# A new written order of five engines' work in the prologue of a fused cross-attention and quantized FFN kernel

## The reference, cut to what matters

```python
h = _layernorm(x)
q, k, v = proj(h, Wq, bq), proj(ctx, Wk, bk), proj(ctx, Wv, bv)      # 16 heads of 32
p = softmax(clip(where(attend, clip(q @ k.T / sqrt(32), -50, 50), -1e4), -50, 50))
delta = clip(residual_scale, 0, 0.3) * ((p @ v) @ Wo.T + bo)
x = x + tanh(g_xattn[0]) * (_layernorm(delta) * ln_gamma + ln_beta)
u = _layernorm(x)
# bit_linear: tokens rounded to 8-bit codes by their own maximum, weights to {-1, 0, 1} times mean(|w|)
gate, val = silu(bit_linear(u, gate_w, gate_b)), bit_linear(u, val_w, val_b)     # 512 -> 2048
return x + tanh(g_ffn[0]) * bit_linear(gate * val, out_w, out_b)                 # 2048 -> 512
```

## Time and profile before

| what | value |
|---|---|
| median of 3 runs | 716.33 us (715.44 to 716.71) |
| the profiled execution | 714.52 us |
| its span, first to last instruction | 712.7 us |
| TensorE busy | 665.8 us, 93% of the span |
| VectorE busy | 586.1 us, 82% |
| ScalarE busy | 497.7 us, 70% |
| GpSimd busy | 311.1 us, 44% |
| mean granted TensorE clock | 0.978 of full |

### The profile page before, as it was taken

How to read it: one execution, slowest core, us unless ns; L and a number is a source line. 1 busy time by engine, 2 the same in 40 slices (tenths; PEclk the granted TensorE clock), 3 DMA queues, 4 the chain that set the end, 5 groups by cost and what they waited for, 6 DMA issues and landing times.

```text
span 712.7 us, 14015 instructions
## 1 busy us (share of the span) xinstructions
PE 665.8 (93%) x4555; PEld 320.1 (45%) x4566; DVE 586.1 (82%) x1226; ACT 497.7 (70%) x660; POOL 311.1 (44%) x483
## 2 busy tenths in 40 slices
PE   4899656979999999999999999999999999999997
PEld 4435435434444454445444544454444444454444
DVE  5888798887877977898888887888779877879986
ACT  3487789679657975787668767786579656964444
POOL 2310315234644465445635473456535643363530
PEclk9999885999999999999999999999999999999999
DMA  9884545031742356236543545336433731363212
GB/s 328 236 283 158 121 184 160 4 74 39 152 113 68 84 132 136 62 77 127 115 97 88 118 103 118 88 84 137 100 75 75 162 75 44 61 127 93 64 45 75
DMA packets 170231, 79.84 MB, mean 112 GB/s; under 512 B 149385, under 2 KB 149713, under 8 KB 169554
## 3 DMA queue, kind: packets, MB, share of 16 engines
q1 hardware_dynamic: 170194, 79.37, 45.4%
HBM read 37.59 MB, written 10.56 MB: 68 GB/s over the span
## 4 chain that ended last, share of the span: by engine, by line
PE 37%; DVE 28%; issue 16%; POOL 6%; DMA 5%; ACT 5%; another core or an unknown queue 1%; SPq 1%; DVEq 0%; POOLq 0%; ACTq 0%
PE psum L1843 11%; PE psum L1906 9%; PE psum L1897 6%; PE psum L1972 4%; DVE arena L1309 3%; DVE hmax L1314 2%; ACT arena L928 2%; DVE xmax L1394 2%; DVE stats L1382 2%; DMA arena<-arena 2%; DMA arena<-x_both 2%; DMA arena<-in_L_xattn_Wq 2%; DVE arena L1412 1%; POOL arena L699 1%
## 5 line engine op out<-in xcount | busy, mean ns | idle before, releaser
L1843 PE MATMUL psum<-ternary,xqT 128*128 128x512 f16 x1024 | 240.2, 383 | 0.0
L1843 PEld LDWEIGHTS psum<-ternary,xqT 128*128 128x128 f16 x1024 | 95.0, 99 | 117.8 <-issue 14.6
L888 ACT ACTIVATE arena<-psum,dequant 128x512 f32<-128x512 f32 x128 | 86.5, 681 | 45.6 <-PE psum L1843 31.9
L1897 PE MATMUL psum<-ternary,arena 128*128 128x512 f16 x496 | 116.1, 379 | 2.4 <-DMA arena<-arena 2.4
L691 POOL TENSOR_TENSOR rstd<-var_e,minus_half 128x1 f32<-128x1 f32 x64 | 40.1, 626 | 162.0 <-DVE var_e L1360 85.5
L1309 DVE SCALAR_TENSOR_TENSOR arena<-psum,dequant,arena 128x512 f32<-128x512 f32 x105 | 78.1, 744 | 13.2 <-ACT arena L888 11.9
L1906 PE MATMUL psum<-wo_hi,arena 128*128 128x512 f16 x256 | 81.4, 379 | 2.0 <-ACT arena L943 1.9
L1314 DVE TENSOR_REDUCE hmax<-arena 128x1 f32<-128x1024 f32 x64 | 77.6, 1212 | 0.5
L1906 PE MATMUL psum<-arena,wq_hi 128*128 128x512 f16 x256 | 76.2, 379 | 1.2 <-DMA arena<-x_both 0.8
L1897 PEld LDWEIGHTS psum<-ternary,arena 128*128 128x128 f16 x496 | 45.9, 98 | 59.4 <-issue 9.7
L928 ACT ACTIVATE arena<-arena,round_c 128x1024 f16<-128x1024 f32 x62 | 70.9, 1144 | 0.6 <-DVE arena L1333 0.6
(11 more groups left out here) (211 smaller groups left out, 1175.3 us busy)
## 6 DMA issues: line engine op xcount, KB each, us to landing
arena<-in_x SPq DMA_DIRECT2D x64, 256.0 KB, 2.8
out<-arena SPq DMA_DIRECT2D x31, 256.0 KB, 2.3
...
arena<-arena SPq DMA_TRANSPOSE x90, 3.1
...
```

What stands on the lines that cost most here:

```text
L888: A.activation(gs[:, t % 2, n * CW:(n + 1) * CW], psG[n % 2], ACT.Silu, scale=dequant[:, t, 0:1]).then_inc(silu_done.sem, 1)
L1843: ins = M.matmul(ps[:], xqT[:, t % 2, k, :], w[:, k, cols], start=(not begun and k == 0), stop=(k == KC - 1 and i != 2))
L1897: ins = M.matmul(psO[:], hidT[t % 2][:, k, :], wo2[:, k, :], start=(k == 0), stop=(k == FC - 1))
```

## The change

Only the order of calls changes, in the setup part, in `first_row`, `first_tile` and `second_tile` of PE, DVE and ACT, in POOL's `first_row`, and in SP's list of DMAs. No operation is added or removed, the choice of the engine for each stays, and rows from tile 2 of row 0 on keep their order. The diff, cut to its core (loops that are written out line by line with the same order are left out):

```diff
 # SP, setup
-            for c in range(W_CHUNKS):
-                load_w(0, c)
             for t in range(2):
                 sp.wait_ge(s_h0_tr, t + 1)
                 sp.dma_start(xa[:, t, :], x[1, t * P:(t + 1) * P, :]).then_inc(xa_loaded[t].sem, 16)
+            load_w(0, 0)
+            load_w(0, 1)
+            load_w(0, 2)
+            load_w(0, 3)
             load_w(1, 0)
             load_w(1, 1)
             sp.wait_ge(s_pe, TURN["ctx", KC - 1] + 1)
             load_w(1, 2)
+            sp.wait_ge(s_pe, TURN["values", KC - 1] + 1)
+            load_w(1, 3)
             sp.wait_ge(s_bpart, PARTS)
...
             load_keys(0)
...
-            sp.wait_ge(s_pe, TURN["values", KC - 1] + 1)
-            load_w(1, 3)
 # ACT, setup
-            sum_abs(0, 2)
-            values(0)
-            sum_abs(0, 3)
-            values(1)
-            sum_abs(1, 0)
...
+            values(0)
+            values(1)
+            sum_abs(1, 0)
+            first_h_high(3)
...
             values(2)
-            sum_abs(1, 1)
             values(3)
 # ACT, first_row
+                    round_w(0, 0)
                     query(0)
...
+                    sum_abs(1, 1)
                     query(2)
...
                     h_high(1, 1)
-                    round_w(0, 0)
                     c_high(0)
...
                     weight_copy(0, 0)
-                    weight_copy(0, 2)
-                    sum_abs(1, 3)
+                    round_w(1, 0)
                     round_input(0, 0)
...
+                    sum_abs(2, 3)
+                    weight_copy(0, 2)
+                    weight_copy(0, 4)
                     h_high(1, 3)
-                    round_w(1, 0)
+                    weight_copy(0, 6)
                     inverse_rows(0, 0)
 # DVE, setup
             V.tensor_reduce(amax1[:, 3:4], kmax[:], AX, ALU.max).then_inc(s_amax1, 1)
-            first_h_low(3)
-            for t in range(2):
-                x_stats(1, t)
             row_max(3)
 # DVE, first_row
-                    weight_copy(0, 1)
-                    weight_copy(0, 3)
...
                     weight_round(0, 3)
                     weight_clip(1, 0)
+                    weight_copy(0, 1)
+                    weight_copy(0, 3)
+                    weight_round(1, 1)
                     weight_copy(0, 5)
                     weight_copy(0, 7)
-                    weight_round(1, 1)
+                    weight_clip(1, 2)
 # DVE, second_tile
                     hidden(1, 0)
-                    new_x(0, 2)
+                    hidden(1, 1)
                     x_shift(2, 1)
                     weight_copy(2, 4)
-                    hidden(1, 1)
+                    new_x(0, 2)
+                    weight_copy(2, 6)
 # PE, setup
             transposes("wq", wq_raw, s_wq, 16)
+            weight_total(0)
             transposes("wo", wo_raw, s_wo, 16)
-            weight_total(0)
 # PE, first_row
-                    project(0, 1)
-                    weight_total(1)
-                    xq_transpose(0, 0)
...
+                    weight_transpose(1, 5)
                     wait(pe, d_ready, 0, 1)
+                    project(0, 1)
+                    weight_transpose(1, 6)
+                    weight_transpose(1, 7)
 # PE, first_tile
                     gate_val(0, 2)
+                    gate_val(0, 3)
                     query(2)
                     weight_transpose(2, 2)
-                    gate_val(0, 3)
+                    weight_transpose(2, 3)
                     query(3)
                     pe.wait_ge(*copied(2, 1))
                     xq_transpose(0, 1)
-                    weight_transpose(2, 3)
 # PE, second_tile
                     project(0, 2)
+                    weight_transpose(2, 4)
+                    weight_transpose(2, 5)
                     gate_val(1, 0)
-                    weight_transpose(2, 4)
                     gate_val(1, 1)
-                    weight_transpose(2, 5)
+                    gate_val(1, 2)
                     weight_transpose(2, 6)
-                    gate_val(1, 2)
                     weight_transpose(2, 7)
                     gate_val(1, 3)
...
                     down(0, 0, range(0, DOWN_AT_SCORES[1]))
+                    down(0, 0, range(*DOWN_AT_SCORES[1:]))
                     scores(1)
-                    down(0, 0, range(*DOWN_AT_SCORES[1:]))
                     xq_transpose(0, 2)
```

227 lines of the change are left out of this document (123 added, 104 removed).

## The result

The changed kernel takes 707.34 us (median of 4 runs, 706.31 to 708.37), the one before 715.88 us beside it (4 runs, 714.04 to 716.71): ratio 0.988, 95% interval 0.9854 to 0.9907, so 8.5 us less. Measured a second time it was 708.77 us (6 runs, 706.78 to 711.02) against 716.14 us (11 runs), 0.9895 (0.9871 to 0.9919). The forecast was 710.5 us, with 707.0 to 716.0 as its range: right in direction, while the gain came out 1.6 to 2.7 us larger than the 5.8 us that were forecast.

The account below looks back on a forecast made before the run. TensorE, 98% busy behind gate_val(2, 0), was taken as the bound, so the question was when it gets there. Stage terms -1.1 - 0.2 - 4.5 = -5.8 turned 714.52 into 708.7 us, median 710.5, range 707.0 to 716.0.

Parts of the forecast that it names:

- The frame: From gate_val(2, 0) of row 0 on, TensorE is 98% busy, so work starting earlier by d should end earlier by d.
- First stage, -1.1 us: Up to the start of weighted(0), 80.62 us before: waits that go or come make it 1.1 us shorter.
- ScalarE's two long operations between the queries: First stage: round_w(0, 0) and sum_abs(1, 1) take back more than the slack there, an estimated 0.5 us.
- the late keys: Rival: the kcur load queues behind the bias stores, scores(0) 3 to 4 us late; sum -1.2, 715.1 us; chance 0.08.
- Second stage, -0.2 us: From weighted(0) to the biases of gate_val(0, 0), 40.40 us before: 0.2 us shorter, with project(0, 1) at full clock.
- The rival in which it is on the path at the half clock: Second stage: ScalarE's late copies and project(0, 1) cost +2.6 instead of -0.2; 713.3 us; chance 0.25.
- Third stage, -4.5 us: From the biases of gate_val(0, 0) to gate_val(2, 0), 49.66 us before: waits and half clock removed, 4.5 us shorter.
- (1): First tile: the 1.88 us wait for query(3) falls to 0.5, a new 0.9 us wait comes; gain 0.5.
- (2): Second tile: the 2.30 us wait for VectorE's copy goes and the quarter behind it runs at full clock; gain 3.8.
- (3): First quarter of the first tile at the full clock, with project(0, 1) close ahead; gain 1.65.
- (4): The tail: down ahead of scores(1) delays the last four exps, and inverse_rows(0, 2) comes ahead of h_high; cost 0.3.
- the walk: Third stage estimate of 5.65 us, taking each handover as short as the shortest; 1.15 us was kept back.

Follow-up runs that it names:

- f1: The changed kernel itself, measured again: 708.77 us.
- e5: The kernel before with the changed setup alone, on all engines and in the DMA order: 715.44 us.
- e2: The kernel before with first_tile and second_tile alone in the changed order: 709.34 us.
- e1: The changed kernel with first_tile and second_tile of TensorE, VectorE and ScalarE put back to the old order: 711.09 us.
- e4: The changed kernel with second_tile alone put back on TensorE, ScalarE and VectorE: 708.82 us.
- e7: The changed kernel with second_tile of TensorE, ScalarE and VectorE and first_tile of VectorE alone put back: 711.23 us.
- f3: The changed kernel with keys(0) on TensorE ahead of largest_in_a_row(0) and largest_to_all(0), and VectorE's row_max(0) and scale_up(0) moved later: 707.38 us.
- e8: The changed kernel with VectorE's first_c_low(3) and weight_round(0, 3) ahead of x_shift(1, 3), and ScalarE's round_w(1, 2), weight_copy(0, 2) and (0, 4) earlier: 707.42 us.
- f2: e8 with GpSimd's update_resid(0, 0) and the first half of update_start(0, 1) held until all 16 gate and value transposes are done: 705.90 us.
- e6: The changed kernel with project(0, 1) on TensorE moved between xq_transpose(0, 0) and weight_transpose(0, 5): 709.22 us.

## Why the prediction was right or wrong

- **The frame held.** Behind `gate_val(2, 0)` the kernel is 542.0 to 542.7 us long in every profile. A gain ahead of it reached the end whole.
- **First stage, -1.1 us: -1.18 in the pair of profiles, but that agreement is partly luck.** Neither execution had a fall of the clock. Without one the changed setup and first row give 79.3 to 79.8 us (six profiles), the old 80.62, so about -1.1 is right for undisturbed executions. The text saw no such falls and gave no bound for them; f1, with two, is 3.75 us longer. The gain is the setup's (e5 beside f1), so ScalarE's two long operations between the queries cost nothing at `weighted(0)`, where the text took 0.5 us. The low bound of this stage, -2.1, adds that cost as if it were a gain; its terms give -1.6. `row_max(3)` comes 1.05 us earlier (46.23 us, 47.28 before), where the term kept 0.7.
- **SP's order and the late keys:** the rival fell. The bias stores are issued at 56.74 us and take 2.98 us, not 9.79, and `kcur` is issued at 66.29 us (SP's queue after); no wait for it stands ahead of `scores(0)`.

```profile
56.74 2.98 SPq L631 DMA_DIRECT2D bias_scratch<-bias_cut  x3
...
66.29 1.59 SPq L491 DMA_DIRECT2D kcur<-ternary  x1
```

- **Second stage, -0.2 us: -0.48 and -0.32.** Old lists gave 40.40, 40.93 and 40.95 us (before, e2, e5), the changed ones 39.90 to 40.16 (changed, f1, e1, e4, e7) and 40.79 in f3, whose attention was slow: a gain of 0.2 to 1.1 us without f3. No run divides it. The mechanism was right: `project(0, 1)` stands in the gap and is hidden at the full clock. The rival in which it is on the path at the half clock fell. VectorE's waits for TensorE at `weight_copy(1, 3)` and `(1, 5)`, put at 1.1 us each at the half clock, were 0.42 and 0.20 us, and the 5.17 us ahead of the run of 40 transposes were a wait for VectorE's copy, not for ScalarE's. The claim that the number of meetings of VectorE with GpSimd stays as it is was not exact: no rounding or clip of VectorE is above 1.3 us in the first profile (2.18 before), one is 1.92 us in f1. It cost nothing there: f1's stage is 0.16 us longer, but 0.11 us shorter from `weight_total(1)` on. Where VectorE's list has no wait left, as in e8, such a meeting is worth 0.6 us (f2).
- **Third stage, -4.5 us: -6.68. This term was the furthest off.** Its parts against what the rows give: (1) up to the end of the first tile, without the first quarter, forecast 0.5. The waits came nearly as walked, 0.59 us for `query(3)` and 0.79 us for the new one (0.9 forecast). From the biases of `gate_val(0, 0)` to those of `gate_val(1, 0)` it went from 26.95 to 24.85 us (145.12 - 119.36, less 0.91 for two groups of transposes that moved in, by the two that take 151.06 to 151.97 us), so 2.10, of which 1.75 is the first quarter: 0.35 for this part. (2) The wait of 2.30 us and the quarter behind it, forecast 3.8: from the biases to `scores(0)` 13.95 us before, 9.81 now with the 0.91 added: 4.14. (3) The first quarter with its biases at the full clock, forecast 1.65: 1.75 (3.82 us before, 2.07 now). (4) The tail, forecast as a loss of 0.3: from `scores(0)` to the end of the stage 8.76 us before and 8.32 now, a gain of 0.44, as `scores(1)` now follows `down` without a wait (0.36 us before). The sum is 6.68 where the walk had 5.65, and the 1.15 us kept back for slack that the walk had missed did not exist. Of the error of 2.2 us half is that reserve, laid over a walk that had already named each wait, and a third (0.74) the sign of the tail.
- **What was luck in this stage:** the text took both quarters at the half clock (3.2 us) as following from the order. In e5, with the same lists and waits, 3.0 us of it were not lost. Had the profile of before been like that one, the third stage would have gained 3.7 us, under the 4.5 that were forecast. The medians (7.4 and 8.5 us) show that the whole gain does not hang on that one profile; how often the old order loses these 3.0 us, three profiles (before, e2, e5) can't say.
- **Where the mechanism was misplaced:** the text put the 3.8 us down to the order of the second tile's transposes together with the earlier copies. e4 shows that the second tile's own order is worth 1.17 us in all. The cause is the first tile, as the sentence on `hidden(0, 1)` and `input_scale(0, 1)` had it: VectorE's list there holds 2.23 us of waits, and the rest of the first tile's 3.63 us is the clock behind the wait.
- **The clock:** the Trainium skill, TensorE: Matmul & The Clock Gate, section What's actually happening, has activity release the throttle; e6 agrees, since with the same work one gap earlier the tile began at 1.2 GHz. I said that this rule leans neither way. It leaned to the change: work put into the last gap was worth 1.9 us.

What stays open: why a fall comes in one execution and not in the next where the waits ahead of it are alike (`values(2)` in f1 and in f2 both follow a wait of 0.37 us; only f1 has a further 0.27 us ahead of it); and which of the setup's edits hold the first stage's 1.1 us.
